# Hashed experts: token rows turned in 32x32 blocks by VectorE, with their quarters loaded on four partition groups

## Chip, cores and metric

The kernel runs on one core of a Trainium2 chip. The metric is the device time in microseconds of one execution; the time given is the median of three runs. The profile is one execution taken by the hardware profiler.

## What is computed

The whole kernel is two layers, each an add of the residual around a conditioned mixture and a second block. The change touches the second layer's mixture only, which picks the expert of a token by a hash:

```
xk = x + dxprev * time_maa_k
e_idx = token_ids * HASH_PRIME % E                       # E = 16 experts
expert_in = buf[:E * C].reshape(E, C, D)                 # C = 256 rows of D = 512 each, scattered from xk
h = square(relu(einsum('ecd,edf->ecf', expert_in, w_key)))       # F = 1024
expert_out = einsum('ecf,efd->ecd', h, w_value)
```

All data is fp32. A product is made of three matmuls on the parts hi and lo of both operands (hi is the operand rounded to fp32r, lo is what is left).

## The kernel before

The program goes through stages, each with its own queues on the engines: shared expert, routed experts, choice, FFN, hashed experts, recurrence. The stages follow each other with a meeting of all engines between them.

**FFN stage.** For each of 32 batches of 128 tokens, POOL computes `xk` in `mix` (L1487; of the last batch VectorE does it in `last_mix`, L1687) and scatters its 128 rows of 2 KB into `hash_in` in DRAM, sorted by expert (L1491). At its end SP loads the first expert's 256 rows as two loads of 128 rows, one row per partition (L1443, `store_r`).

**Hashed stage** (`stage_hashed`). A software pipeline goes over the 16 experts; each engine has a list of stages with a lag, written out by hand, and works through it in that order in each step. `x` holds an expert's rows, `x[:, m]` the 128 rows of half m, with channels along the free axis. TensorE needs channels on partitions, so in step e:

- SP loads w1 of expert e (2 MB, L1902; it waits until w1_lo of the expert before is made), then the two halves of x (L1894; each waits for the semaphore `tx0` or `tx1`, so for its buffer to have been turned), stores half 1 of expert e-2, loads w2 of expert e, a piece of the gate weights, and stores half 0 of e-1.
- TensorE does up(0) to up(3) of expert e-1 (96 matmuls of 256 columns into `h_ps`), then `turn_x(0)` and `turn_x(1)` of expert e (eight 128x128 transposes into the PSUM tiles `tx_ps`, L2077), then down(0) and down(1) of expert e-1 (48 matmuls of 512 columns into `o_ps`). down(0) waits before its chunks k = 0, 2, 4, 6 for w2_lo and for `h_lo(0)`, (1), (2), (3); up(0) waits for both `x_lo` and for all of w1_lo.
- ScalarE makes the hi parts, the relu (`pos`) and the copies out; VectorE the squares (`relu2`, L2031) and the lo parts: `h_lo` (L2037), `x_lo` (L2044), `w1` and `w2` (L2019). Its order is g_lo, w2(0,2), relu2(0), w2(2,3), relu2(1), h_lo(0), w2(3,4), relu2(2), h_lo(1), relu2(3), h_lo(2), h_lo(3), x_lo(0), x_lo(1), w1(0,4).
- In the last step `load_ahead` brings weights of the recurrence into `staged`, and `turn_state` (L2108) turns the first state into `tx_ps[0]`, after `x_lo0`.

Of the kernel before, what the change touches and what calls it, by code (L numbers as in the profile page):

```python
# [13 lines left out]
P = 128  # L14
# [80 lines left out]
def product(pe, out, a, w, first, last):  # L95


    (a_hi, a_lo), (w_hi, w_lo) = a, w
    pe.matmul(out, a_hi, w_hi, start=first, stop=False, skip_group_check=True)  # L99
    pe.matmul(out, a_hi, w_lo, start=False, stop=False, skip_group_check=True)  # L100
    return pe.matmul(out, a_lo, w_hi, start=False, stop=last, skip_group_check=True)  # L101


# [1195 lines left out]
def stage_ffn(nc, ins, d, keep):  # L1299


    with ExitStack() as ctx:
# [80 lines left out]
        def _(sp):  # L1383
# [53 lines left out]
            def store_r(i, n, turn):  # L1437
                b = batch(sp, i)
                if is_last(i):
                    sp.wait_ge(S["mm2"], NB)  # L1440
                    sp.wait_ge(S["xk_sent"], 16 * NB)
                    for m in range(2):
                        sp.dma_start(keep["s5_x"][:, m], d["hash_in"][m * P:(m + 1) * P]).then_inc(S[f"first_hash{m}"], 16)  # L1443
                sp.wait_ge(S["r_ready"], i + 1)
                sp.dma_start(d["r"][b], r[:]).then_inc(S["r_out"], 16)
# [6 lines left out]
        def _(pool):  # L1452
# [21 lines left out]
            def mix(i, n, turn):  # L1474
                if not (isinstance(i, int) and i == NB - 1):
                    pool.wait_ge(S["prev_in"], i * 48 + 48)
                    pool.tensor_tensor(dx[:], prev[:], x1[:], ALU.subtract).then_inc(S["dx"], 1)
                    pool.wait_ge(S["dx"], i + 1)
                    pool.tensor_tensor(k_part[:], dx[:], maa_r[:], ALU.mult).then_inc(S["r_part"], 1)
                    pool.wait_ge(S["r_part"], i + 1)  # L1480
                    wait_for(pool, S["txr"], i)
                    pool.tensor_tensor(xr[:], k_part[:], x1[:], ALU.add).then_inc(S["xr"], 1)
                    pool.wait_ge(S["xr"], i + 1)
                    pool.tensor_tensor(k_part[:], dx[:], maa_k[:], ALU.mult).then_inc(S["k_part"], 1)
                    pool.wait_ge(S["k_part"], i + 1)
                    wait_for(pool, S["xk_sent"], i * 16)
                    pool.tensor_tensor(xk[:], k_part[:], x1[:], ALU.add).then_inc(S["xk"], 1)  # L1487
                pool.wait_ge(S[f"hrec_in{n}"], turn * 16 + 16)
# [112 lines left out]
        def _(dve):  # L1601
# [76 lines left out]
            def last_mix(i, n, turn):  # L1678
                if is_last(i):
# [6 lines left out]
                    dve.wait_ge(S["xk_sent"], (NB - 1) * 16)  # L1686
                    dve.tensor_tensor(xk[:], k_part[:], x1[:], ALU.add).then_inc(S["xk"], 1)  # L1687
                    dve.wait_ge(S["xk"], NB)
# [142 lines left out]
def stage_hashed(nc, ins, d, keep):  # L1831

    with ExitStack() as ctx:  # L1833
        sb = lambda n, s, t=FP32: ctx.enter_context(nc.sbuf_tensor("s5_" + n, s, t))
        ps = lambda n, s, t=FP32: ctx.enter_context(nc.psum_tensor("s5_" + n, s, t))
        S = sems(nc, ctx, "s5_", "w1_in w2_in w1_hi w1_lo w2_hi w2_lo tx0 tx1 x_hi0 x_hi1 x_lo0 x_lo1 "
                 "g_in g_hi g_lo h_ps pos relu h_hi h_lo mm2 o_ready0 o_ready1 ~o_out0 ~o_out1 "
# [29 lines left out]
        NST = 4  # L1867
        staged = right("staged", [P, NST, HS])
        w2_lo = sb("w2_lo", [P, DC, HS], FP32R)

# [7 lines left out]
        h_ps = [ps(f"h_ps{q}", [P, 2, CAP]) for q in range(NQ)]  # L1878
        tx_ps = [ps(f"tx_ps{n}", [P, DC, P]) for n in range(2)]
        o_ps = [ps(f"o_ps{n}", [P, D]) for n in range(2)]  # L1880
# [7 lines left out]
        def _(sp):  # L1888
            def load_x(m):
                def stage(e):  # L1890
                    if isinstance(e, int) and e == 0:
                        return
                    wait_for(sp, S[f"tx{m}"], e)
                    sp.dma_start(x[:, m], d["hash_in"][bass.ds(e * CAP + m * P, P)]).then_inc(S[f"x_in{m}"], 16)  # L1894
                return stage
# [15 lines left out]
            def load_ahead(e):  # L1911
                if isinstance(e, int) and e == EH - 1:
                    sp.wait_ge(F["r_out"], 16 * NB)
                    sp.dma_start(staged[:], ins["gate_w"][0:NST].rearrange("u p n -> p u n")).then_inc(S["u_in"], 16)
                    sp.dma_start(first_rec[:], d["rec"][0]).then_inc(S["rec_in"], 16)
                    for m in range(2):
                        sp.wait_ge(S[f"tx{m}"], EH)
                    sp.dma_start(first_c[:], ins["in_c"].partition_broadcast(P)).then_inc(S["c_in"], 16)
# [20 lines left out]
        def _(act):  # L1939
# [15 lines left out]
            def x_hi_(m):  # L1955
                def stage(e):
                    act.wait_ge(S[f"tx{m}"], e + 1)
                    wait_for(act, S["h_ps"], NQ * e)
                    act.activation(x_hi[:, :, rows(m)], tx_ps[m][:], ACT.Copy).then_inc(S[f"x_hi{m}"], 1)
                return stage  # L1960
# [36 lines left out]
            def state_hi(e):  # L1997
                if isinstance(e, int) and e == EH - 1:
                    act.wait_ge(S["c_turned"], 1)
                    act.wait_ge(S["h_ps"], EH * NQ)  # L2000
                    act.activation(keep["c_hi"][:], tx_ps[0][:], ACT.Copy).then_inc(S["c_hi"], 1)

# [9 lines left out]
        def _(dve):  # L2012
# [21 lines left out]
            def h_lo(q):  # L2034
# [4 lines left out]
                return stage  # L2039

            def x_lo_(m):
                def stage(e):
                    dve.wait_ge(S[f"x_hi{m}"], e + 1)
                    dve.tensor_tensor(x_lo[:, :, rows(m)], tx_ps[m][:], x_hi[:, :, rows(m)],  # L2044
                                      ALU.subtract).then_inc(S[f"x_lo{m}"], 1)
# [11 lines left out]
            def state_lo(e):  # L2057
                if isinstance(e, int) and e == EH - 1:
                    dve.wait_ge(S["c_hi"], 1)
                    dve.tensor_tensor(keep["c_lo"][:], tx_ps[0][:], keep["c_hi"][:], ALU.subtract)  # L2060

# [4 lines left out]
                (1, unit_lo(0, 1)), (1, relu2(2)), (1, h_lo(1)), (1, unit_lo(1, 2)), (1, relu2(3)), (1, h_lo(2)),  # L2066
                (1, h_lo(3)), (1, unit_lo(2, 4)), (1, state_lo), (1, unit_lo(4, UNITS)), (0, x_lo_(0)), (0, x_lo_(1)),
                (0, w1(0, 4))])

        @block.tensor  # L2070
        def _(pe):
            def turn_x(m):
                def stage(e):
                    pe.wait_ge(S[f"x_in{m}"], e * 16 + 16)
                    wait_for(pe, S[f"x_lo{m}"], e)
                    for k in range(DC):
                        mm = pe.transpose(tx_ps[m][:, k], x[:, m, k * P:(k + 1) * P], ident[:])  # L2077
                    mm.then_inc(S[f"tx{m}"], 1)
                return stage

            def up(q):
# [26 lines left out]
            def turn_state(e):  # L2108
                if isinstance(e, int) and e == EH - 1:
                    pe.wait_ge(S["c_in"], 16)  # L2110
                    pe.wait_ge(S["x_lo0"], EH)
                    for k in range(DC):
                        mm = pe.transpose(tx_ps[0][:, k], first_c[:, k * P:(k + 1) * P], ident[:])
                    mm.then_inc(S["c_turned"], 1)

            software_pipeline(pe, EH, [
                (1, up(0)), (1, up(1)), (1, up(2)), (1, up(3)), (1, turn_state), (0, turn_x(0)), (0, turn_x(1)), (1, down(0)),
                (1, down(1))])

# [438 lines left out]
```

## Time and profile before

| | us |
|---|---|
| median of 3 runs | 2510.55 (2509.78 to 2514.25) |
| span of the profiled execution | 2502.9 |
| difference of the two | 7.65 |

The profiled execution's own time outside of its span isn't recorded; the 7.65 us above are between its span and the median of the runs.

| engine | busy us | share of the span |
|---|---|---|
| TensorE matmul | 2451.8 | 98% |
| TensorE weight load | 2046.1 | 82% |
| VectorE | 1148.3 | 46% |
| ScalarE | 897.2 | 36% |
| GpSimd (POOL) | 551.4 | 22% |

The hashed stage runs from about 1466 to 1848 us. Engines are PE (TensorE), PEld (its weight loads), DVE (VectorE), ACT (ScalarE), POOL (GpSimd), SP; SPq is the queue on which SP issues DMAs. A profile shows what an engine was busy with, and in brackets how long it sat idle before and what ended that. An average busy share mixes stages with different limits: what a change in the hashed stage does has to be read from that stage.

### The profile page before, as it was taken

The page shows a single profiled execution, that of the slowest core. Times are in us where ns is not written, and L with a number is a line of the kernel's source. Part 1 is how long each engine was busy: PE and PEld are TensorE (multiplying, and loading weights), DVE is VectorE, ACT ScalarE, POOL GpSimd, SP SyncE. Part 2 cuts the span into 40 slices and gives each one's busy share as a digit, 9 for nine tenths or more (in the row PEclk, how much of TensorE's full clock was granted, in tenths as well). Part 3 has the DMA queues.
Part 4 walks back from the last instruction along what each step waited for, and adds up shares of the span by engine and source line. Part 5 has one row for each costly group of instructions (what it writes and reads, how often), then busy time and mean ns, then how long its engine had stood idle before and what let it go on. Part 6 is the DMA issues. An engine that isn't in the chain of part 4 may idle for free. (4 is left out here: it accounts for less than half of the span.)

```text
span 2502.9 us, 40913 instructions
## 1 busy us (share of the span) xinstructions
PE 2451.8 (98%) x12556; PEld 2046.1 (82%) x12557; DVE 1148.3 (46%) x1771; ACT 897.2 (36%) x1459; POOL 551.4 (22%) x498
## 2 busy tenths in 40 slices
PE   8999999999999899999999989999999999999999
PEld 4778888888899688888888878998978888888877
DVE  5655555325343344344434356766643333332356
ACT  2233333216555222222222246666642222222234
POOL 1100000002222276666657510000011111111100
PEclk9999999999999999999999999999999999999999
DMA  8698898317466433363343266665641011110025
GB/s 297 210 329 310 301 318 317 141 44 269 150 238 223 172 120 111 114 255 108 113 171 127 92 235 230 239 227 222 241 141 43 25 34 30 29 34 25 25 101 185
DMA packets 135988, 412.81 MB, mean 165 GB/s; under 512 B 29843, under 2 KB 34419, under 8 KB 119394
## 3 DMA queue, kind: packets, MB, share of 16 engines
q1 hardware_dynamic: 108626, 314.20, 35.3%
q0 software_dynamic: 19072, 61.66, 7.7%
q10 hardware_dynamic: 8208, 35.88, 3.7%
q8 instruction: 47, 0.77, 0.1%
q14 instruction: 35, 0.29, 0.0%
HBM read 558.71 MB, written 144.80 MB: 281 GB/s over the span
## 5 line engine op out<-in xcount | busy, mean ns | idle before, releaser
L99 PE MATMUL s_g<-wx_hi,s_x_hi 128*128 128x512 f32 x512 | 203.4, 397 | 2.3 <-DVE s_x_lo L2306 1.6
L101 PE MATMUL s_g<-wx_hi,s_x_lo 128*128 128x512 f32 x512 | 200.2, 391 | 0.0
L100 PE MATMUL s_g<-wx_lo,s_x_hi 128*128 128x512 f32 x512 | 199.5, 390 | 0.0
L2019 DVE TENSOR_TENSOR s_w_lo<-s_w_raw,s_w_hi 128x1024 fp32r<-128x1024 f32 x124 | 146.4, 1222 | 75.3 <-ACT s_w_hi L1948 73.7
L99 PE MATMUL s_g<-s_u,s_c_hi 128*128 128x512 f32 x384 | 152.8, 398 | 1.6 <-PEq L1833 1.6
L101 PE MATMUL s_g<-s_u,s_c_lo 128*128 128x512 f32 x384 | 149.9, 390 | 0.0
L100 PE MATMUL s_g<-s_u,s_c_hi 128*128 128x512 f32 x384 | 149.5, 389 | 0.0
L99 PE MATMUL s_h_ps<-s_x_hi,s_w_hi 128*128 128x256 f32 x512 | 144.9, 283 | 1.7 <-DVE s_x_lo L2044 1.7
L101 PE MATMUL s_h_ps<-s_x_hi,s_w_lo 128*128 128x256 f32 x512 | 144.9, 283 | 0.0
L100 PE MATMUL s_h_ps<-s_x_lo,s_w_hi 128*128 128x256 f32 x512 | 144.9, 283 | 0.0
L2205 POOL DMA_INDIRECT s_y<-mid_hash_out,first_rec x32 | 31.6, 986 | 475.4 <-DMA mid_hash_out<-s_o 392.8
L2291 DVE TENSOR_TENSOR s_gate<-s_g,s_bias 128x512 f32<-128x512 f32 x96 | 66.1, 691 | 137.1 <-PE s_g L101 137.1
L1948 ACT ACTIVATE s_w_hi<-s_w_raw 128x1024 fp32r<-128x1024 f32 x124 | 124.1, 1053 | 5.7 <-DMA s_w_raw<-in_w2h 5.7
L394 ACT ACTIVATE s_sg_h<-s_gate 128x512 f32<-128x512 f32 x64 | 38.1, 597 | 245.4 <-PE s_up L101 245.3
L2235 ACT ACTIVATE s_gate<-s_gate 128x512 f32<-128x512 f32 x96 | 60.4, 632 | 175.1 <-DVE s_gate L2291 175.1
L2211 POOL TENSOR_TENSOR s_x<-s_y,s_r 128x512 f32<-128x512 f32 x32 | 44.0, 1374 | 357.4 <-ACT s_r L2223 343.6
L655 DVE TENSOR_TENSOR s_sg_h<-s_sg_h,s_up 128x512 f32<-128x512 f32 x64 | 43.9, 688 | 168.8 <-ACT s_sg_h L394 168.6
L99 PEld LDWEIGHTS s_g<-wx_hi,s_x_hi 128*128 128x128 f32 x512 | 96.2, 188 | 22.5 <-DVE s_x_lo L2306 2.1
L99 PE MATMUL s_gate<-s_xt_hi,s_w_hi 128*128 128x512 f32 x256 | 102.7, 401 | 11.7 <-DVE s_w_lo L472 9.9
L101 PEld LDWEIGHTS s_g<-wx_hi,s_x_lo 128*128 128x128 f32 x512 | 96.1, 188 | 20.9
L100 PEld LDWEIGHTS s_g<-wx_lo,s_x_hi 128*128 128x128 f32 x512 | 96.3, 188 | 19.4 <-issue 0.2
L1555 ACT ACTIVATE s_z_hi<-s_tz_ps 128x512 fp32r<-128x512 f32 x32 | 19.2, 599 | 248.6 <-PE s_tz_ps L1755 248.6
(411 smaller groups left out, 6814.0 us busy)
## 6 DMA issues: line engine op xcount, KB each, us to landing
s_half<-mid_w ACTq DMA_DIRECT2D x124, 2048.0 KB
s_w_raw<-in_w SPq DMA_DIRECT2D x64, 512.0 KB, 6.2
mid_w<-s_x_grp SPq DMA_DIRECT2D x32, 1024.0 KB, 5.8
mid_w<-s_pool_b SPq DMA_DIRECT2D x32, 1024.0 KB, 4.9
s_half<-mid_w SPq DMA_DIRECT2D x32, 1024.0 KB
s_w_raw<-in_w2h SPq DMA_DIRECT2D x16, 2048.0 KB, 7.4
s_w_raw<-in_w1h SPq DMA_DIRECT2D x15, 2048.0 KB, 7.4
mid_routed<-s_o_sb SPq DMA_DIRECT2D x72, 256.0 KB
```

Of the source, the lines that this page charges most:

```text
L99: pe.matmul(out, a_hi, w_hi, start=first, stop=False, skip_group_check=True)
L100: pe.matmul(out, a_hi, w_lo, start=False, stop=False, skip_group_check=True)
L101: return pe.matmul(out, a_lo, w_hi, start=False, stop=last, skip_group_check=True)
L394: act.activation(sg[:, c % 2], gate_ps[c % banks][:], ACT.Silu).then_inc(S["silu"], 1)
L655: dve.tensor_tensor(h[:, c % 2], sg[:, c % 2], up_ps[c % banks][:], ALU.mult).then_inc(S["hmul"], 1)
L1555: act.activation(dst[:], src[:], ACT.Copy).then_inc(S[name], 1)
L1948: act.activation(hi[:, c], raw[:, c], ACT.Copy).then_inc(S[name + "_hi"], 1)
L2019: dve.tensor_tensor(lo[:, c], raw[:, c], hi[:, c], ALU.subtract).then_inc(S[name + "_lo"], 1)
L2205: pool.indirect_dma_start(y[:], None, d["hash_out"], bass.IndirectOffsetOnAxis(rec[:, SLOTH:SLOTH + 1].bitcast(U32), 0)).then_inc(S["y_in" ...
L2211: pool.tensor_tensor(x2[:], y[:], r[:], ALU.mult).then_inc(S["x2"], 1)
L2235: act.activation(gate[:, g], gate[:, g], f).then_inc(S["acted"], 1)
L2291: dve.tensor_tensor(gate[:, g], g_ps[n][g][:], bias[:, g], ALU.add).then_inc(S["added"], 1)
```

## The change

The rows of an expert are no longer turned by TensorE.

- `xk` is written with its columns in another order: quarter g of a row holds columns 32g to 32g+31 of all four 128-column chunks (`by_quarter`), on POOL, and on VectorE for the last batch.
- A half of x is loaded by four DMAs of 32 partitions each, one for each quarter g. Partition 32g + t takes from rows t, 32+t, 64+t, 96+t their quarter g: runs of 512 bytes for 2 KB. They all count on one semaphore (64 for a half in place of 16).
- VectorE's `transpose` of such a tile turns its 32x32 blocks and leaves the channel-major layout in `xt`, in SBUF. `xt` lies on a part of `staged`.
- `turn_x` goes from TensorE's list, where it stood ahead of down(0), to VectorE's, between h_lo(2) and h_lo(3). `x_hi` and `x_lo` read `xt` in SBUF in place of `tx_ps` in PSUM.
- `load_ahead` waits for both `x_lo` of the last expert before it loads `staged`; before, it waited for `tx0` and `tx1`, behind that load. `turn_state` has a PSUM tile of its own, `tc_ps`, and doesn't wait for `x_lo0` any more.

```diff
+def load_by_quarters(eng, dst, rows, sem):
+
+    for g in range(P // 32):
+        eng.dma_start(dst[32 * g:32 * g + 32].rearrange("t (s c) -> t s c", c=P),
+                      rows[:, g * P:(g + 1) * P].rearrange("(s t) c -> t s c", t=32)).then_inc(sem, 16)
+
+
+def in_order(row):
+    return row.rearrange("p (k g a) -> p k g a", k=DC, g=4)
+
+
+def by_quarter(row):
+
+    return row.rearrange("p (g k a) -> p k g a", g=4, k=DC)
+
+
+def turn_quarters(dve, dst, src):
+
+    return dve.transpose(dst.rearrange("p k (s t) -> p k s t", t=32), src.rearrange("p (s k a) -> p k s a", s=4, a=32))
...
-                        sp.dma_start(keep["s5_x"][:, m], d["hash_in"][m * P:(m + 1) * P]).then_inc(S[f"first_hash{m}"], 16)
+                        load_by_quarters(sp, keep["s5_x"][:, m], d["hash_in"][m * P:(m + 1) * P], S[f"first_hash{m}"])
...
-                    pool.tensor_tensor(xk[:], k_part[:], x1[:], ALU.add).then_inc(S["xk"], 1)
+                    pool.tensor_tensor(by_quarter(xk[:]), in_order(k_part[:]), in_order(x1[:]), ALU.add).then_inc(S["xk"], 1)
...
-                    dve.tensor_tensor(xk[:], k_part[:], x1[:], ALU.add).then_inc(S["xk"], 1)
+                    dve.tensor_tensor(by_quarter(xk[:]), in_order(k_part[:]), in_order(x1[:]), ALU.add).then_inc(S["xk"], 1)
...
+        xt = staged[:, 0].rearrange("p (k n) -> p k n", k=DC)
...
-        tx_ps = [ps(f"tx_ps{n}", [P, DC, P]) for n in range(2)]
+        tc_ps = ps("tc_ps", [P, DC, P])
...
-                    wait_for(sp, S[f"tx{m}"], e)
-                    sp.dma_start(x[:, m], d["hash_in"][bass.ds(e * CAP + m * P, P)]).then_inc(S[f"x_in{m}"], 16)
+                    wait_for(sp, S[f"xt{m}"], e)
+                    load_by_quarters(sp, x[:, m], d["hash_in"][bass.ds(e * CAP + m * P, P)], S[f"x_in{m}"])
...
                     sp.wait_ge(F["r_out"], 16 * NB)
+                    for m in range(2):
+                        sp.wait_ge(S[f"x_lo{m}"], EH)
                     sp.dma_start(staged[:], ins["gate_w"][0:NST].rearrange("u p n -> p u n")).then_inc(S["u_in"], 16)
                     sp.dma_start(first_rec[:], d["rec"][0]).then_inc(S["rec_in"], 16)
-                    for m in range(2):
-                        sp.wait_ge(S[f"tx{m}"], EH)
...
-                    act.wait_ge(S[f"tx{m}"], e + 1)
+                    act.wait_ge(S[f"xt{m}"], e + 1)
                     wait_for(act, S["h_ps"], NQ * e)
-                    act.activation(x_hi[:, :, rows(m)], tx_ps[m][:], ACT.Copy).then_inc(S[f"x_hi{m}"], 1)
+                    act.activation(x_hi[:, :, rows(m)], xt[:, :, rows(m)], ACT.Copy).then_inc(S[f"x_hi{m}"], 1)
...
+            def turn_x(m):
+                def stage(e):
+                    dve.wait_ge(S[f"x_in{m}"], e * 64 + 64)
+                    wait_for(dve, S[f"x_lo{m}"], e)
+                    turn_quarters(dve, xt[:, :, rows(m)], x[:, m]).then_inc(S[f"xt{m}"], 1)
+                return stage
...
-                    dve.tensor_tensor(x_lo[:, :, rows(m)], tx_ps[m][:], x_hi[:, :, rows(m)],
+                    dve.tensor_tensor(x_lo[:, :, rows(m)], xt[:, :, rows(m)], x_hi[:, :, rows(m)],
...
-                (1, h_lo(3)), (1, unit_lo(2, 4)), (1, state_lo), (1, unit_lo(4, UNITS)), (0, x_lo_(0)), (0, x_lo_(1)),
+                (0, turn_x(0)), (0, turn_x(1)), (1, h_lo(3)), (1, unit_lo(2, 4)), (1, state_lo), (1, unit_lo(4, UNITS)), (0, x_lo_(0)), (0, x_lo_(1)),
...
-            def turn_x(m):
-                def stage(e):
-                    pe.wait_ge(S[f"x_in{m}"], e * 16 + 16)
-                    wait_for(pe, S[f"x_lo{m}"], e)
-                    for k in range(DC):
-                        mm = pe.transpose(tx_ps[m][:, k], x[:, m, k * P:(k + 1) * P], ident[:])
-                    mm.then_inc(S[f"tx{m}"], 1)
-                return stage
...
-                    pe.wait_ge(S["x_lo0"], EH)
...
-                (1, up(0)), (1, up(1)), (1, up(2)), (1, up(3)), (1, turn_state), (0, turn_x(0)), (0, turn_x(1)), (1, down(0)),
+                (1, up(0)), (1, up(1)), (1, up(2)), (1, up(3)), (1, turn_state), (1, down(0)),
```

## Rows read from the trace of the kernel before

**Rows 1.** Windows: busy time and count per engine in one step, clock, DMA share, GB/s
```profile
1693.00:1716.60 23.60, 23.60 (x155) 21.44 (x153) 16.26 (x19) 14.63 (x21) 0.00 (x0) 1.00 0.61 230
```
**Rows 2.** Chain that ended last: start, us, what; two steps
```profile
1693.30 0.87 PE s_tx_ps L2077 x8
...
1716.88 0.87 PE s_tx_ps L2077 x8
```
**Rows 3.** Timeline of TensorE (start, us, instruction), from up to down to up
```profile
1693.01 0.28 PE L101 MATMUL s_h_ps<-s_x_hi,s_w_lo 128*128 128x256 f32 x1
...
1693.13 1.03 PE L2077 MATMUL s_tx_ps<-ident,s_x 128*128 128x128 f32 x8
...
1693.92 0.48 PE L99 MATMUL s_o_ps<-s_w_hi,s_ht_hi 128*128 128x512 f32 x1
...
1694.24 0.39 PE L100 MATMUL s_o_ps<-s_w_lo,s_ht_hi 128*128 128x512 f32 x1
...
1705.20 0.28 PE L99 MATMUL s_h_ps<-s_x_hi,s_w_hi 128*128 128x256 f32 x1
```
**Rows 4.** Timeline of VectorE: first expert, then the same step as rows 3
```profile
1483.00 1.47 DVE L2037 TENSOR_TENSOR s_ht_lo<-s_h,s_ht_hi 128x512 fp32r<-128x512 f32 x2
...
1694.05 0.69 DVE L2031 TENSOR_TENSOR s_h<-s_pos,s_h_ps 128x512 f32<-128x512 f32 x1 [1.59 <-ACT s_pos L1966]
1694.66 1.48 DVE L2037 TENSOR_TENSOR s_ht_lo<-s_h,s_ht_hi 128x512 fp32r<-128x512 f32 x2
1696.05 1.28 DVE L2044 TENSOR_TENSOR s_x_lo<-s_tx_ps,s_x_hi 128x512 fp32r<-128x512 f32 x2
1697.36 4.63 DVE L2019 TENSOR_TENSOR s_w_lo<-s_w_raw,s_w_hi 128x1024 fp32r<-128x1024 f32 x4
```
**Rows 5.** Timeline of ScalarE in that step
```profile
1694.77 0.63 ACT L1973 ACTIVATE s_ht_hi<-s_h 128x512 fp32r<-128x512 f32 x1 [0.32 <-DVE s_h L2031]
```
**Rows 6.** Timeline of VectorE and TensorE in the last expert, where TensorE waits
```profile
1837.05 0.68 DVE L2031 TENSOR_TENSOR s_h<-s_pos,s_h_ps 128x512 f32<-128x512 f32 x1
1837.65 1.47 DVE L2037 TENSOR_TENSOR s_ht_lo<-s_h,s_ht_hi 128x512 fp32r<-128x512 f32 x2
...
1838.48 0.47 PE L99 MATMUL s_o_ps<-s_w_hi,s_ht_hi 128*128 128x512 f32 x1 [0.47 <-DVE s_ht_lo L2037]
1838.79 0.39 PE L100 MATMUL s_o_ps<-s_w_lo,s_ht_hi 128*128 128x512 f32 x1
```
**Rows 7.** Timeline of SP's queue, and DMA issues (count, KB each, us to landing)
```profile
1702.69 0.86 SPq L1894 DMA_DIRECT2D s_x<-mid_hash_in  x2
...
s_x<-mid_hash_in SPq DMA_DIRECT2D x30, 256.0 KB, 7.7
```
**Rows 8.** Start of the stage: timelines, and the landing of L1443's two loads
```profile
1460.07 0.83 SPq L1443 DMA_DIRECT2D s_x<-mid_hash_in  x2
...
DMA to landing us min/median/max: 2.6/2.8/2.9
...
1466.28 1.06 PE L2077 MATMUL s_tx_ps<-ident,s_x 128*128 128x128 f32 x8 [1.75 <-PEq L1302]
...
1466.94 1.09 ACT L1959 ACTIVATE s_x_hi<-s_tx_ps 128x512 fp32r<-128x512 f32 x2 [1.78 <-PE s_tx_ps L2077]
...
1469.01 0.36 PE L99 MATMUL s_h_ps<-s_x_hi,s_w_hi 128*128 128x256 f32 x1 [1.66 <-DVE s_x_lo L2044]
```
**Rows 9.** Windows around the stage's start, columns as rows 1
```profile
1457.00:1460.00 3.00, 0.74 (x5) 0.51 (x5) 3.00 (x4) 2.26 (x3) 0.86 (x1) 1.00 0.47 175
1460.00:1462.00 2.00, 2.00 (x6) 1.59 (x7) 2.00 (x2) 0.23 (x1) 0.00 (x0) 0.61 0.37 110
...
1464.00:1469.00 5.00, 1.60 (x11) 0.97 (x10) 1.29 (x2) 1.68 (x3) 0.00 (x0) 1.00 0.50 147
```
**Rows 10.** Timeline of POOL in the FFN stage
```profile
1198.46 1.30 POOL L1487 TENSOR_TENSOR s_xk<-s_k_part,s_x 128x512 f32<-128x512 f32 x1 [0.16 <-POOL s_k_part L1484]
...
1204.44 0.96 POOL L1460 DMA_INDIRECT s_routed<-mid_routed,s_rec  x1 [2.78 <-DVE s_y_part L1643]
```

More of the change, by code:

```diff
@@ L1835, in stage_hashed @@
         ps = lambda n, s, t=FP32: ctx.enter_context(nc.psum_tensor("s5_" + n, s, t))
-        S = sems(nc, ctx, "s5_", "w1_in w2_in w1_hi w1_lo w2_hi w2_lo tx0 tx1 x_hi0 x_hi1 x_lo0 x_lo1 "
+        S = sems(nc, ctx, "s5_", "w1_in w2_in w1_hi w1_lo w2_hi w2_lo xt0 xt1 x_hi0 x_hi1 x_lo0 x_lo1 "
                  "g_in g_hi g_lo h_ps pos relu h_hi h_lo mm2 o_ready0 o_ready1 ~o_out0 ~o_out1 "
@@ L2000, in state_hi @@
                     act.wait_ge(S["h_ps"], EH * NQ)
-                    act.activation(keep["c_hi"][:], tx_ps[0][:], ACT.Copy).then_inc(S["c_hi"], 1)
+                    act.activation(keep["c_hi"][:], tc_ps[:], ACT.Copy).then_inc(S["c_hi"], 1)
             w1 = lambda c0, c1: split_w("w1", w1_raw, w1_hi, "h_ps", NQ, c0, c1)
@@ L2059, in state_lo @@
                     dve.wait_ge(S["c_hi"], 1)
-                    dve.tensor_tensor(keep["c_lo"][:], tx_ps[0][:], keep["c_hi"][:], ALU.subtract)
+                    dve.tensor_tensor(keep["c_lo"][:], tc_ps[:], keep["c_hi"][:], ALU.subtract)
             w1 = lambda c0, c1: split_w("w1", w1_raw, w1_hi, w1_lo, c0, c1)
@@ L2110, in turn_state @@
                     pe.wait_ge(S["c_in"], 16)
-                    pe.wait_ge(S["x_lo0"], EH)
                     for k in range(DC):
-                        mm = pe.transpose(tx_ps[0][:, k], first_c[:, k * P:(k + 1) * P], ident[:])
+                        mm = pe.transpose(tc_ps[:, k], first_c[:, k * P:(k + 1) * P], ident[:])
                     mm.then_inc(S["c_turned"], 1)
             software_pipeline(pe, EH, [
-                (1, up(0)), (1, up(1)), (1, up(2)), (1, up(3)), (1, turn_state), (0, turn_x(0)), (0, turn_x(1)), (1, down(0)),
+                (1, up(0)), (1, up(1)), (1, up(2)), (1, up(3)), (1, turn_state), (1, down(0)),
                 (1, down(1))])
```

## The prediction

> **What bounds the kernel now.** I read the windows first: in one expert's step of the hashed stage TensorE is busy 23.60 of 23.60 us at full clock, VectorE 16.26, ScalarE 14.63 [rows 1]. The chain of the end comes back in every step to the eight transposes of `turn_x` [rows 2]. So TensorE alone sets the step, and what leaves its queue is won unless something else becomes late. The timeline then gives the step's parts [rows 3]: the last up matmul starts at 1693.01, the transposes at 1693.13, the first down matmul at 1693.92, the next at 1694.24, and the next expert's up, 47 down matmuls on, at 1705.20. Down matmuls follow each other every (1705.20 - 1694.24)/47 = 0.233 us; the one behind the transposes takes 0.32, which is 0.09 more. From 1705.20 the next 96 up matmuls take about 11.5 us, and the period is 23.58 (the two chain rows).
>
> **Removed from TensorE.** 1693.92 - 1693.13 = 0.79 us of transposes, plus the 0.09 after them if the 128-column transposes cause it: 0.79 to 0.88 per step, I take 0.87, since 0.233 is what each of the 46 others takes. Sixteen pairs of transposes exist; the first stands alone at the stage's start, fifteen lie between an up and a down.
>
> **Added to VectorE, and what waits for it.** Two turns now stand between `h_lo(2)` and `h_lo(3)`, and down(0) needs `h_lo(3)` for its chunks k=6 and 7. Before, `relu2(3)` starts at 1694.05 and `h_lo(2)` at 1694.66 [rows 4]; back to back such instructions follow each other every 0.60 to 0.61 us though each shows 0.68 (1837.05 to 1837.65, [rows 6]), so the next slot is at 1694.66 + 0.61 = 1695.27. ScalarE's `h_hi(3)` ends by 1694.77 + 0.63 = 1695.40 [rows 5] and is out of the way. With T for one turn, `h_lo(3)` ends at 1695.27 + 2T + 0.68. TensorE answers 0.14 us later: `h_lo(2)` of the last expert ends at about 1837.65 + 0.68 = 1838.33 and the matmul that waited starts at 1838.48; that one also takes 0.31 to the next, 0.08 too long [rows 6]. So the matmul is possible at 1696.09 + 2T. It is due, with the transposes gone, 18 matmuls after 1693.13: 1693.13 + 18 x 0.233 = 1697.33. The stall per step is 2T - 1.24, plus 0.08 if it is above zero: 2T - 1.16.
>
> No VectorE transpose is in the profile. Lower end: a turn costs what any 128x512 instruction does, 0.61. Upper end: twice the columns' time, as a 128x1024 instruction, (4.63 us for four) 1.16 [rows 4]. I take 0.65, near the lower row, because it reads and writes the same 512 elements per partition; the surplus 0.04 is for filling and emptying the blocks. The stall is then 0.14 and the net gain 0.87 - 0.14 = 0.73 per step.
> The Trainium skill ("VectorE: DVE Perf Modes", The three transpose paths) gives 311 ns for a 128x128 bf16 transpose on VectorE, in 32x32 blocks. With the columns of a 1x instruction (the rows' 1.16 less 0.61 for 512 columns, 1.07 ns each) 311 ns is 137 for the columns and 174 of fixed cost, near the 0.68 - 0.55 = 0.13 of our rows, so by it the turn would show 0.72 and pass in 0.65 if fp32 goes as fast as bf16; no run here shows that yet. The same page's rules for kernel authors send a 128x128 transpose to TensorE when PSUM will do; by that rule the change gives up 0.79 us of TensorE for at least 1.22 of VectorE, and the sum goes by which of the two is waited for.
>
> **The first two steps.** In the first expert VectorE runs late: `h_lo(2)` starts at 1483.00, 2.5 us after the end of the up phase and not 1.5 as later [rows 4]. TensorE would be due for k=6 at 1469.01 + 96 x 0.12 + 4.2 = 1484.7; `h_lo(3)` would be ready at 1483.61 + 1.30 + 0.68 + 0.14 = 1485.7. The stall of 1.0 eats the 0.87: this step gives nothing. At the stage's start the transposes (1466.28) give `x_hi` at 1466.94 and the first up matmul at 1469.01 [rows 8]. With turns from the same moment, the second ends at 1467.6, `x_hi(1)` at 1468.3, `x_lo(1)` at 1469.0, up starts at 1469.15: 0.15 late.
>
> **Sum.** 14 steps x 0.73 = 10.2; step one 0; start -0.15: 10.0 us less. The trace has only the span (2502.9); the runs' median is 2510.55, 7.65 above it, and their three values spread over 4.5. I take the difference off the median: 2500.5 (span 2492.9).
>
> **What I cost at nothing, and its cover.** (1) w1's low halves now end later: `h_lo(3)` slot ends 1697.2, two `x_lo` 1698.4, four `w1_lo` (4.63, [rows 4]) 1703.1. Up is due at 1693.13 + 0.14 + 11.2 = 1704.5: 1.3 us of cover, 3 before; without it each late us costs 15. ScalarE's `x_hi` now reads SBUF, and its four w1 copies start about 1 us later; they stay ahead of VectorE's, which are slower. (2) SP: two loads of 256 KB become eight of 64 KB. Both took 0.86 us to issue, 0.43 each [rows 7]; eight take 3.4. They stand behind w1 and ahead of `store(1)`, w2 and gate loads. w1 goes out about 1.1 us later (its gate is `w1_lo`), the pieces from 1703.8 to 1707.3, and landing at the 7.7 of [rows 7], most of which is w1's own 2 MB ahead of them, 1715.0. The turn wants them at 1695.27 + 22.85 = 1718.1: cover 3.1 us. What stands behind in SP's queue (`store(1)`) has a whole step before its buffer is reused. On VectorE the turn's wait holds `h_lo(3)`, `x_lo` and w1, and with them TensorE: nothing if the cover holds. Packets of 512 B for 2 KB cost between nothing and four times the landing of a load alone: 2.8 [rows 8] to 11.2, 8.4 more, which would pass the cover. I take under 1, because these loads spend most of their time behind w1. (3) The first eight loads start at 1460.07 and are issued by 1463.5, landed by 1466.4 with 2.9 [rows 8], the moment the turns begin; the r store behind them in SP's queue waits for TensorE's last products anyway. (4) `xk` is written in runs of 32 elements: POOL takes 1.30 for it now and idles 2.78 ahead of its next gather [rows 10]; between no change and twice (+1.3) nothing waits. The last batch's is VectorE's, 0.69, on the path: 0 to 0.1. (5) The staged load now waits for `x_lo` of the last expert, done 9 us before SP gets there behind `store(1)`. (6) `turn_state` has its own bank and one wait less; its four transposes stay.
>
> **Rivals.**
> *A, forecast*: 2500.5; with T from 0.61 to 0.75 the steps give 0.81 to 0.53, hence 2499.2 to 2503.3. Chance 0.45.
> *B, the clock falls at the start.* At 1460 to 1462 the granted clock was 0.61 (between the levels 1.2 and 2.4 GHz), after TensorE had been busy 0.74 of 3.00 us; at 1464 to 1469 it held 1.00 with 1.60 of 5.00 busy, 1.06 of it the transposes that go [rows 9]. Without them 0.54 of 5.15 remains. A fall costs what it did there, matmuls 0.42 apart for about 3.3 us, 8 x 0.19 = 1.5 us: 2502.0. Chance 0.20.
> The Trainium skill ("TensorE: Matmul & The Clock Gate", Part 4) says transposes do not count as TensorE being busy in the same way; by it the clock would do now as it did before, and B falls. The rows can't separate the two.
> *C, slower: the turn takes twice as long.* The gain is gone when 2T - 1.16 = 0.87, T = 1.01. At T = 1.16 the stall is 1.16 and each of 14 steps loses 0.29 (4.1), step one another 1.2, the start 1.2, likely with B's 1.5: 8 us, 2518.5. For it: 4-byte data turned in blocks with a strided source, shown nowhere here. Against: the same bytes in and out as its neighbours. Chance 0.12.
> *D, slower: the pieces land late.* From 3.1 us beyond the old landing each us costs 15; at the far bound, (8.4 - 3.1) x 15 = 80, 2590. Against: the DMA share of a step is only 0.61 [rows 1]. Chance 0.05.
> The Trainium skill ("DMA: Bandwidth & Descriptors", Measured) calls transfers under 64 KB descriptor-dominated and asks for large ones; by it the pieces at 64 KB are at the edge, and D is what it would do here.
> *E, the gain is smaller:* the turn at 0.85 to 0.95, or TensorE's switch of sizes keeps its 0.09 and waking costs more: 0.1 to 0.4 per step, 2505 to 2509. Chance 0.18.
>
> **Range and chances.** Faster by over 0.2% (5.0 us, about what a measurement can tell from no change) means below 2505.5: A, B and some of E, 0.68. Within: most of E, and little of C, 0.17. Slower: most of C and D, 0.15. 2498.5 to 2510 holds A, B and E, leaves out C and D.
>
> **What would show it.** In the profile after: no `s_tx_ps` matmuls at the old line, chain and step period 22.85 in place of 23.58; VectorE's turns 0.7 us long, `h_lo(3)` ending at 4.1 us after the up phase's end; TensorE idle about 0.15 a step before k=6, released by `s_ht_lo`; up never waiting for `w_lo`; VectorE never waiting for DMA before a turn. A turn above 1.0, a wait for `s_x`, or up waiting for w1 makes the prediction wrong; a fallen clock near 1469 moves it to B.

## The result, and the profile after

| | before | after |
|---|---|---|
| median, us | 2511.51 (2509.78 to 2514.25, 4 runs) | 2496.77 (2495.91 to 2497.94, 4 runs) |
| ratio | | 0.9945, interval 0.9931 to 0.9958 |
| span of the profiled execution, us | 2502.9 | 2494.3 |
| period of the hashed stage, us | 23.58 | 22.72 |

The kernel got 14.7 us faster; 10.0 had been forecast, and 2496.77 lies below the range. The direction and the place are as predicted, the size isn't. Of the runs that are quoted further on, one of the changed kernel took 3496.12 us at a mean granted clock of 0.65 in place of 0.99; no ratio counts it.

The windows of the kernel after, in one step of the hashed stage; columns as in [rows 1]:

```profile
1693.00:1715.70 22.70, 22.70 (x146) 20.45 (x145) 17.27 (x23) 14.81 (x22) 0.00 (x0) 1.00 0.68 236
```

TensorE is still busy in all of it. VectorE rose from 16.26 to 17.27. The timeline of TensorE, from the up matmuls to the first down matmul and on to the next up, answers [rows 3]:

```profile
1689.49 0.28 PE L101 MATMUL s_h_ps<-s_x_hi,s_w_lo 128*128 128x256 f32 x1
1689.61 0.39 PE L99 MATMUL s_o_ps<-s_w_hi,s_ht_hi 128*128 128x512 f32 x1
1689.84 0.39 PE L100 MATMUL s_o_ps<-s_w_lo,s_ht_hi 128*128 128x512 f32 x1
...
1700.80 0.28 PE L99 MATMUL s_h_ps<-s_x_hi,s_w_hi 128*128 128x256 f32 x1
```

The first down matmul comes 0.12 us behind the last up matmul; it was 0.91 before (1693.92 - 1693.01). The next follows after 0.23, not 0.32. So the 0.79 of transposes and most of the 0.09 behind them are gone. The waits of TensorE from 1440 to 1850 us (engine, what it was to do, what it waited for: total, times, longest) show no wait that comes back in every step:

```profile
PE s_h_ps L99 <- DVE s_x_lo L2073: 4.6, 1, 4.6
...
PE s_o_ps L99 <- DVE s_ht_lo L2059: 0.5, 1, 0.5
```

The second stands in the last expert, as it did before [rows 6]. VectorE's timeline in the same step answers [rows 4]:

```profile
1690.53 0.69 DVE L2053 TENSOR_TENSOR s_h<-s_pos,s_h_ps 128x512 f32<-128x512 f32 x1 [1.59 <-ACT s_pos L1988]
1691.13 0.69 DVE L2059 TENSOR_TENSOR s_ht_lo<-s_h,s_ht_hi 128x512 fp32r<-128x512 f32 x1
1691.74 1.30 DVE L122 STREAM_TRANSPOSE s_staged<-s_x 128x512 f32<-128x512 f32 x2
1692.96 0.65 DVE L2059 TENSOR_TENSOR s_ht_lo<-s_h,s_ht_hi 128x512 fp32r<-128x512 f32 x1
1693.53 1.28 DVE L2073 TENSOR_TENSOR s_x_lo<-s_staged,s_x_hi 128x512 fp32r<-128x512 f32 x2
1694.73 4.62 DVE L2041 TENSOR_TENSOR s_w_lo<-s_w_raw,s_w_hi 128x1024 fp32r<-128x1024 f32 x4
```

The two turns take the queue for 1692.96 - 1691.74 = 1.22 us, 0.61 each. `h_lo(3)` ends at 1693.61 and TensorE could go on 0.14 later, at 1693.75. The down matmul that needs it is the 19th, due at 1689.61 + 18 x 0.233 = 1693.80. By these ends it fits with 0.05 us to spare. The matmul itself does start when it is due, but the one behind it doesn't:

```profile
1693.80 0.42 PE L99 MATMUL s_o_ps<-s_w_hi,s_ht_hi 128*128 128x512 f32 x1
1694.06 0.39 PE L100 MATMUL s_o_ps<-s_w_lo,s_ht_hi 128*128 128x512 f32 x1
```

It follows after 0.26 in place of 0.23. The same 0.26 or 0.27 stands behind the first matmul of k=6 in every step from the third to the fifteenth. So the slack is used up, and a first 0.02 to 0.03 of a stall shows.

### Where the two traces differ

I put anchors into both traces and measured between them: the last batch's `x1` on VectorE in the FFN stage (an instruction that the change leaves alone), the first up matmul, the first down matmul, the second expert's up, the last expert's up, and the recurrence's first matmul.

| stretch, us | before | after | difference |
|---|---|---|---|
| start to `x1` of the last batch | 1450.37 | 1452.66 | +2.29 |
| to the first up | 18.64 | 18.77 | +0.13 |
| to the first down | 12.70 | 13.72 | +1.02 |
| to the second expert's up | 11.28 | 11.18 | -0.10 |
| 14 steps | 330.11 | 318.09 | -12.02 |
| last up to the recurrence | 25.63 | 25.66 | +0.03 |
| recurrence to the end | 654.17 | 654.22 | +0.05 |

Fourteen steps give 12.0; the forecast had 10.2 there. The spans differ by only 8.6, since this trace of before is of a short execution: 2502.9 of span where its runs take 2511.5, while the time outside the span is 1.6 (2495.91 for a span of 2494.3 after), and not the 7.65 between this span and the median. Two rows of the table, 2.29 and 1.02, therefore had to be told from the change. The second is TensorE's clock, in the windows of after (answering [rows 9]):

```profile
1471.00:1473.00 2.00, 1.57 (x7) 1.60 (x8) 0.28 (x1) 0.00 (x0) 0.00 (x0) 0.50 0.99 418
...
1475.00:1477.00 2.00, 2.00 (x14) 2.00 (x14) 0.00 (x0) 0.40 (x1) 0.00 (x0) 0.68 1.06 451
```

After an idle stretch of 4.6 us the first up matmuls run at the lower level, 1.2 GHz, 0.21 apart, where they ran 0.12 apart in the trace of before. That looks like rival B. Whether the change causes it is what the first three experiments ask.

### The profile page after: what moved, and what is told of

It reads as the page before. It is cut to its first block and busy times, and to the rows that moved or that the text cites. A ratio compares the mean times of both kernels' runs of the same rounds, so it can differ in the third digit from the quotient of the medians.

```text
span 2494.3 us, 40938 instructions
## 1 busy us (share of the span) xinstructions
PE 2440.2 (98%) x12427; PEld 2033.9 (82%) x12429; DVE 1165.9 (47%) x1803; ACT 900.0 (36%) x1459; POOL 552.1 (22%) x498
## 5 line engine op out<-in xcount | busy, mean ns | idle before, releaser
L99 PE MATMUL s_gate<-s_xt_hi,s_w_hi 128*128 128x512 f32 x256 | 103.0, 402 | 12.9 <-DVE s_w_lo L493 9.9
```

## The experiments

The first theory (theory 1 in the expectations) was that the gain is the whole of TensorE's 0.86 us per step, with VectorE's turns just fitting in, and that what is seen at the stage's start belongs to the executions and not to the change. Against it stood that the missing transposes let the clock fall (B), that part of the gain comes from the loads or from other places than TensorE's queue, and that the stall of 2T - 1.24 + 0.08 is there but hidden by something else.

### The two kernels again, and the transposes put back

The kernel before ran once more as it is, so did the changed kernel, and a third kernel is the changed one with eight transposes (of the identity, into a spare PSUM tile) in TensorE's queue at their old place:

```diff
+            def spare_turns(e):
+                for m in range(2):
+                    for k in range(DC):
+                        pe.transpose(tc_ps[:, k], ident[:], ident[:])
-                (1, up(0)), (1, up(1)), (1, up(2)), (1, up(3)), (1, turn_state), (1, down(0)),
+                (1, up(0)), (1, up(1)), (1, up(2)), (1, up(3)), (1, turn_state), (0, spare_turns), (1, down(0)),
```

> The kernel before, unchanged, against itself. The traces of before and after differ by 8.6 us in span, the medians of the runs by 14.7; trace by trace, 10.9 of it lies in the hashed stage and 2.3 went the other way ahead of it. Theory 1: the change acts in the hashed stage alone, and the missing 4 us is how much one execution of the same program differs from another ahead of that stage: ratio 1.000 within 0.001, and the spans of the single executions spread over some 4 us, with 2502.9 at their low end. Theory 2: the 14.7 is real and has a part outside of the hashed stage that this trace doesn't show: the spans of before lie close together at about 2509, and a new trace shows where the 4 us are.

> The changed kernel, unchanged, in five rounds. Theory 1 (in-stage effect of 10.9 us only): 11 us under before, ratio 0.9957. Theory 2 (another part outside): 14.7 under it, ratio 0.9942.

> The changed kernel with eight 128x128 transposes of the identity put back on TensorE where turn_x stood (results unused), everything else as changed. Theory 1 (the gain is TensorE's time alone, 0.86 per step with the 0.09 of the switch): the period goes back from 22.72 to 23.58, and the time to that of before, within 1 us. Rival (part of the gain comes from the loads by quarters or from reading SBUF in place of PSUM): the period stays below 23.4 and the time 3 us or more under before.

| | median, us | ratio to before | period | first up to first down |
|---|---|---|---|---|
| before (25 runs beside them) | 2507.97 | | | |
| before again | 2508.38 | 1.0002 (0.9993 to 1.0011) | 23.58 | 15.05 |
| after again | 2495.38 | 0.9952 (0.9938 to 0.9966) | 22.72 | 14.15 |
| after, transposes put back | 2508.94 | 1.0001 (0.9991 to 1.0010) | 23.58 | 14.99 |

The timeline of TensorE in the kernel with the transposes put back, in one step:

```profile
1721.44 1.04 PE L2138 MATMUL s_tc_ps<-ident 128*128 128x128 f32 x8
1722.23 0.48 PE L99 MATMUL s_o_ps<-s_w_hi,s_ht_hi 128*128 128x512 f32 x1
1722.55 0.39 PE L100 MATMUL s_o_ps<-s_w_lo,s_ht_hi 128*128 128x512 f32 x1
```

They bring back 0.79 us and the 0.32 after them, and with these the old period of 23.58 to the hundredth and the old time. The new loads, the turns on VectorE and the other layout of `xk` are all still in that kernel, so together they cost and give nothing that these runs can tell (the interval is 0.1% to each side, 2.5 us; the period is the finer measure). POOL's `xk`, written in runs of 32 elements, takes 1.301 us on average with and without the change, and VectorE's 0.69. The gain is TensorE's time. The unchanged kernel agrees with itself at 1.0002, but its single executions spread from 2503.4 to 2513.4, 10 us and not the 4 that theory 1 had.

The window of the unchanged kernel in its second trace, where its first up matmuls stand:

```profile
1472.00:1474.00 2.00, 2.00 (x11) 2.00 (x11) 0.00 (x0) 0.00 (x0) 0.00 (x0) 0.50 1.00 426
```

The clock falls there too, with eight transposes that start 2.7 us earlier and an idle stretch of 1.67 after them. It held in one execution of this kernel and fell in another; it fell as well with the transposes put back. So the fall comes without the change too, and it doesn't need the transposes to be gone. The Trainium skill ("TensorE: Matmul & The Clock Gate", Part 4) says that transposes don't count as a busy TensorE in the same way; these two traces fit that, the lower level came in spite of eight transposes, but in the first trace of before it didn't come.

Whether the change makes the fall more frequent is another question, and it stays open. The clock fell in all seven traces of kernels that have neither the transposes nor spare matmuls there, and in two of three with the transposes. The mean granted clock of whole runs points the same way, though other stretches enter into it: it is 0.995 or more in 28 of 64 runs of the unchanged kernel, in 3 of 10 with the transposes put back, and in none of 14 of the changed kernel. Against B, the fall isn't the change's alone; as a cost of the change B isn't refuted.

Like for like the first step now reads: 15.05 + 11.28 against 14.15 + 11.17, 1.0 us less. With the 12.0 of the steps and 0.15 to 0.2 lost at the start the stage gains 12.8. Against the execution of before in which the clock held, the changed kernel's first step (24.90 to 25.40 in three traces, 23.98 before) loses 0.9 to 1.4, and the stage gains 10.7 to 10.9.

### The turn's price

Each turn is done twice, the first time into a spare tile; then the same for half 0 alone:

```diff
+        spare = staged[:, 1].rearrange("p (k n) -> p k n", k=DC)
...
+                turn_quarters(dve, spare[:, :, rows(m)], x[:, m])
                 turn_quarters(dve, xt[:, :, rows(m)], x[:, m]).then_inc(S[f"xt{m}"], 1)
```

> The changed kernel with each VectorE turn done twice, the first into an unused tile. By the prediction's working with T = 2 x 0.61, h_lo(3) ends 1.22 later than in the changed kernel, the matmul of k=6 is possible 1.20 after it is due, plus 0.08 for waking: 1.28 per step, 15 steps 19 us, start 1.2: 20 us above the changed kernel, so 5 to 9 above before; TensorE idles at s_ht_lo every step. Rival (VectorE's place in front of h_lo(3) is not what counts, there is more slack than computed): under 5 us above the changed kernel.

> The changed kernel with only the turn of half 0 done twice: 0.61 us more on VectorE per step. With both twice (1.22 more) the period went from 22.72 to 23.90, so the slack ahead of h_lo(3) in the changed kernel would be 1.22 - 1.18 = 0.04 us. If the step is a wait that grows one for one from that slack, the period is 22.72 + 0.61 - 0.04 = 23.29 and the time 8.5 us above the changed kernel. Rival: waking TensorE has a fixed price and the slack is larger; then the period is 23.35 or more, or under 23.2.

All turns twice: 2513.36 us, ratio 1.0024 (1.0014 to 1.0035), 18.0 above the changed kernel of the same comparison; period 23.82 to 23.91. Half 0 twice: 2507.22, ratio 0.9985 (0.9976 to 0.9994), mean period 23.28. TensorE's waits, and then VectorE's timeline, with all turns doubled:

```profile
PE s_o_ps L99 <- DVE s_ht_lo L2060: 15.0, 16, 1.0
```

```profile
1703.33 2.48 DVE L122 STREAM_TRANSPOSE s_staged<-s_x 128x512 f32<-128x512 f32 x4
1705.73 0.65 DVE L2060 TENSOR_TENSOR s_ht_lo<-s_h,s_ht_hi 128x512 fp32r<-128x512 f32 x1
```

The same two views with half 0 doubled:

```profile
PE s_o_ps L99 <- DVE s_ht_lo L2060: 6.1, 16, 0.5
```

```profile
1700.74 1.89 DVE L122 STREAM_TRANSPOSE s_staged<-s_x 128x512 f32<-128x512 f32 x3
1702.56 0.65 DVE L2060 TENSOR_TENSOR s_ht_lo<-s_h,s_ht_hi 128x512 fp32r<-128x512 f32 x1
```

Four turns take 2.40, three 1.82, two 1.22: 0.60 to 0.61 each. The period rises by 0.56 with one turn more (23.28 - 22.72) and by 1.17 with two (mean 23.89), so of the added 0.60 and 1.18 all but 0.04 and 0.01 is paid. From the changed kernel on VectorE's time is paid one for one. This is the stall of the forecast's formula. It exists, and it begins where the change put the kernel. Its two parts show in the traces: with half 0 doubled, in the step of the timeline above, the matmul of k=6 starts at 1703.35, 0.54 after it is due, and the next follows 0.31 later, 0.08 too long:

```profile
1703.35 0.47 PE L99 MATMUL s_o_ps<-s_w_hi,s_ht_hi 128*128 128x512 f32 x1 [0.38 <-DVE s_ht_lo L2060]
1703.66 0.39 PE L100 MATMUL s_o_ps<-s_w_lo,s_ht_hi 128*128 128x512 f32 x1
```

### The turns behind h_lo(3)

If a stall were left in the changed kernel, moving the turns behind `h_lo(3)` would take it away.

```diff
-                (0, turn_x(0)), (0, turn_x(1)), (1, h_lo(3)), (1, unit_lo(2, 4)), ...
+                (1, h_lo(3)), (0, turn_x(0)), (0, turn_x(1)), (1, unit_lo(2, 4)), ...
```

> The changed kernel with both turns on VectorE behind h_lo(3) in place of ahead of it. The slack ahead of h_lo(3) is some 0.04 us in the changed kernel and the stall zero; with the turns behind it the slack is 1.2 us and nothing else waits, so the period stays 22.72 and the time that of the changed kernel within 1 us. Rival: w1_lo, now later still (x_lo waits for x_hi, which waits for the turn), passes its cover of 1.3 us: the period grows.

2498.00 us, ratio 0.9947 (0.9933 to 0.9962), beside 2496.44 and 0.9947 (0.9934 to 0.9959) for the changed kernel in the same comparison. The period is 22.70 against 22.72: 0.3 us in 14 steps. Behind the first matmul of k=6 the next now follows after 0.23 or 0.24, so this 0.02 is what the changed kernel pays of the stall. Nothing more is left to win there. `h_lo(3)` is ready 1.2 us earlier, and the order costs nothing in the period either, though `x_lo` and the w1 copies now wait for ScalarE: the copies end at 1703.53, 0.69 ahead of up at 1704.22, where the changed kernel has 1.45.

> The changed kernel once more, on the chip of the two variants. Theory: the effect in the hashed stage is 12.0 for 14 steps, and 1.0 for step one when the clock is low in both kernels; 12.8 in all, and what a comparison shows beyond is the spread ahead of that stage: ratio 0.995 within 0.001.

### The loads in pieces

The eight pieces of a step become two loads of 128 rows of 2 KB. The layout is left as it then falls, so what the experts are fed is wrong, but every instruction except the loads is the same:

```diff
-    for g in range(P // 32):
-        eng.dma_start(dst[32 * g:32 * g + 32].rearrange("t (s c) -> t s c", c=P),
-                      rows[:, g * P:(g + 1) * P].rearrange("(s t) c -> t s c", t=32)).then_inc(sem, 16)
+    eng.dma_start(dst, rows).then_inc(sem, 16)
...
-                    dve.wait_ge(S[f"x_in{m}"], e * 64 + 64)
+                    dve.wait_ge(S[f"x_in{m}"], e * 16 + 16)
```

> The changed kernel with each half of x loaded by one DMA of 128 rows of 2 KB again, in place of four of 512-byte runs; the rows then lie in the wrong places for the turn, so the expert's input isn't the reference's, and every instruction's size stays. If the pieces cost nothing (they are covered by 3 us and more), period and time are those of the changed kernel within 1 us. Rival: the pieces disturb the stage's start or the w1 load: this kernel is 2 us or more faster.

2499.21 us (2495.22 to 2506.88), ratio 0.9955 (0.9942 to 0.9968), period 22.72. (In its trace the first up stands 0.9 us later behind `x1` than in the changed kernel's, 19.63; one trace doesn't say whether that is the edit or the execution.) The DMA issues from 1500 to 1850 us (what, how many, KB each, us to landing), in pieces and then whole:

```profile
s_x<-mid_hash_in SPq DMA_DIRECT2D x104, 64.0 KB, 6.5
```

```profile
s_x<-mid_hash_in SPq DMA_DIRECT2D x27, 256.0 KB, 7.7
```

The pieces cost nothing that shows: the period is the same to the hundredth and the median not lower (it was expected within 1 us of the changed kernel's, 2496.77, and is 2.4 above it, with runs that spread over 11.7). A piece lands 6.5 us after its issue, a whole load 7.7. The pieces of a step are complete later all the same, since the last is issued 3.7 us after the first; VectorE waits for neither. D is refuted. The Trainium skill ("DMA: Bandwidth & Descriptors", Measured) calls transfers under 64 KB descriptor-dominated; pieces of just 64 KB in runs of 512 B show no price in this kernel.

### The clock at the start

Could the lower clock in the first up phase be bought back? Ten spare matmuls of 512 columns fill TensorE's idle stretch:

```diff
+            for n in range(10):
+                pe.matmul(tc_ps[:].rearrange("p k n -> p (k n)"), w1_hi[:, 0, 0:P], w1_hi[:, 0, 0:D],
+                          start=True, stop=True, skip_group_check=True)
             software_pipeline(pe, EH, [
```

A second kernel has six more at the end of the FFN stage, a third has the ten with the turns behind `h_lo(3)`:

> The changed kernel with ten matmuls of 512 columns (results unused) at the very start of the hashed stage, while VectorE turns. If the clock falls because TensorE idles in the stage's start, the first up matmuls run at 0.12 in place of 0.21: 2.35 us less to the first down, some of it lost because VectorE is then late for k=6 in step one (about 1.0): 1.3 under the changed kernel. Rival: the fall is decided ahead of the stage, in the idle time after the FFN stage's last product: no change, or worse, since the ten matmuls then take 4.3 us and delay up.

> As the kernel with ten spare matmuls at the start of the hashed stage, and six more behind the last product of the FFN stage, in the time in which the engines meet. If the idle time between the stages decides, the clock holds here at 1.00 and the gain of 1.3 to 2.3 under the changed kernel shows; if the clock was lost by then already in the FFN stage's last batch, nothing does.

> Ten spare matmuls at the stage's start, and the turns behind h_lo(3). With the clock held, step one showed a stall: 12.37 us from the first down matmul to up of expert 1, for 11.18. That stall is the turns ahead of h_lo(3) while VectorE is late; behind it, 11.2 to 11.3 should come back, 1.1 us less than with the ten matmuls alone, and 2.4 less than the changed kernel. Rival: the stall is w2's late arrival itself and stays.

| | median, us | ratio to before | `x1` to first up | first up to first down | to second up |
|---|---|---|---|---|---|
| after (its first trace) | 2496.77 | 0.9945 | 18.77 | 13.72 | 11.18 |
| ten spare matmuls | 2496.47 | 0.9944 (0.9929 to 0.9959) | 18.78 | 11.57 | 12.37 |
| with six more ahead | 2498.99 | 0.9950 (0.9936 to 0.9963) | 19.91 | 12.51 | 12.39 |
| ten, turns behind `h_lo(3)` | 2495.85 | 0.9946 (0.9933 to 0.9959) | 18.49 | 12.75 | 12.21 |

The last row stands in a later comparison than the two above it, in which before had 2509.34 and not 2511.01. The kernel with ten: the window of its first up matmuls, TensorE's timeline at the first wait of the down phase, and VectorE's timeline in that step:

```profile
1476.00:1478.00 2.00, 2.00 (x19) 2.00 (x18) 0.00 (x0) 0.00 (x0) 0.00 (x0) 1.00 1.04 438
```

```profile
1488.18 0.47 PE L99 MATMUL s_o_ps<-s_w_hi,s_ht_hi 128*128 128x512 f32 x1 [0.70 <-DVE s_ht_lo L2059]
```

```profile
1480.40 2.36 DVE L2041 TENSOR_TENSOR s_w_lo<-s_w_raw,s_w_hi 128x1024 fp32r<-128x1024 f32 x2 [6.25 <-ACT s_w_hi L1970]
...
1490.37 0.65 DVE L2059 TENSOR_TENSOR s_ht_lo<-s_h,s_ht_hi 128x512 fp32r<-128x512 f32 x1
```

The clock held, and the up phase got 2.15 us shorter. But 1.19 of it is lost again in the down phase, in waits for `h_lo` before k=2 (the line above) and before k=6, where TensorE goes on at 1491.17, 0.15 after the end of `h_lo(3)`. VectorE starts this expert's w2 copies at 1480.40 in any case: they wait for ScalarE's, and these for the first w2, as ScalarE's timeline in this kernel says:

```profile
1479.32 2.01 ACT L1970 ACTIVATE s_w_hi<-s_w_raw 128x1024 fp32r<-128x1024 f32 x2 [5.90 <-DMA s_w_raw<-in_w2h]
```

So with the clock held the first expert is bound by w2's landing. A TensorE that is quicker there waits later. In the third kernel, with the turns out of the way too, TensorE waits for `h_lo` earlier, 1.01 us before its first down matmul and 0.70 before k=2: 12.75 + 12.21 = 24.96 against 13.72 + 11.18 = 24.90. That isn't the work of the order, since the second kernel, with the turns ahead of `h_lo(3)`, has nearly the same two waits (0.76 and 0.70) and 24.90. In both traces w2 came later: ScalarE starts on it 8.9 and 8.7 us after its issue, 7.7 in the trace with ten. Six more spare matmuls in the FFN stage delay the first up by 1.1 us. The ten were expected to give 1.3 us and the third kernel 2.4; no variant is faster than the changed kernel by more than its runs spread.

The same two traces test the first step of the forecast. Clock high in both, [rows 9] and the ten spare matmuls: 12.70 + 11.28 = 23.98 before and 11.57 + 12.37 = 23.94 after. The step gives nothing, as forecast, because the late VectorE eats what is saved. (The 1.13 saved in the up phase is more than 0.87, since in this one execution 1.24 us passed between the last up and the first down matmul, where the other steps have 0.91.) Clock low in both: 1.0 us, because a slower TensorE meets its `h_lo(3)` in time.

## Why the prediction was right, and where it was not

The time came out 3.7 us below the forecast and 1.7 below its range. Of the 3.7, the stall per step, the term that failed, accounts for 1.8, and the first step for 1.0. About 1 is left; the traces don't show it in the hashed stage, and its cause stays open.

**What leaves TensorE: right.** 0.87 forecast, 0.86 measured (23.58 - 22.72), and again 0.86 when the transposes were put back. The 0.09 behind the transposes did belong to them.

**The turn's price and the stall: mechanism right, size off.** This is the term that failed: "2T - 1.16" with T = 0.65, 0.14 per step, 2.0 us in 14. Measured is 0.02 per step, 0.3 us in 14, and no idle time before k=6. Two things were wrong in it. T is 0.61: the turn shows 0.69 and passes in 0.61 like any 128x512 neighbour of it; the 0.04 for "filling and emptying the blocks" had no row behind it. The prediction's estimate from the 311 ns of the Trainium skill ("VectorE: DVE Perf Modes", The three transpose paths) was 0.72 shown and 0.65 spaced if fp32 went as fast as bf16; the trace has 0.686 and 0.61, a little less than that estimate. And the 0.08 for waking TensorE was put into the formula without its condition, though the text named it ("plus 0.08 if it is above zero"): with T = 0.61 the stall is 1.22 - 1.24, just below zero, and but for the 0.02 neither part is paid. The range for A did start at T = 0.61, but 2T - 1.16 gives 0.06 there, and so its 2499.2 was too high: without a stall the same sum gives 2510.55 - 14 x 0.87 + 0.15 = 2498.5. (The 2499.2 also leaves out the 0.15 of the start, which the range's upper end, 2503.3, has.) The runs with three and four turns confirm the slope of the formula, not its constant: against the 22.70 without a stall they add 0.58 and 1.19 to the period, and the formula with their 1.82 and 2.40 on VectorE in place of 2T gives 0.66 and 1.24. It is 0.05 to 0.08 too high, about the price that it sets for waking.

**The first step: right at a high clock, wrong at a low one.** 0 was forecast (0.87 saved, 1.0 waited) from a trace in which the clock held, and with the clock held it is 0.04 (1.13 saved in the up phase, 1.09 lost behind it). It fell in the other trace of before and in every trace of the changed kernel without spare matmuls. With the fall in both kernels the step gives 1.0. I took the clock of one execution at the stage's start for the kernel's.

**The start: right.** 0.15 late forecast; 0.13 in the first pair of traces, 0.18 in the second (18.61 against 18.43).

**The covers: right.** Up waits for no w1: the four copies end at 1699.35 (1694.73 + 4.62), 1.45 ahead of up at 1700.80, 1.3 forecast. The pieces land in time. `xk` costs nothing more on POOL. The issue of the pieces was under-priced, 0.50 each and not 0.43 (SP's queue in the same step, the second line), without consequence:

```profile
1699.51 0.33 SPq L1924 DMA_DIRECT2D s_w_raw<-in_w1h  x1
1700.04 4.01 SPq L107 DMA_DIRECT2D s_x<-mid_hash_in  x8
```

**The rivals.** B: the clock did fall, as the sign said it would, but it falls without the change as well; against an execution of before in which it held, the fall costs 0.9 to 1.4, near the 1.5 of the forecast. C: T is 0.61, not 1.16; the runs with all turns done twice, 1.20 for a pair, show what C would have been: 2513.36, 18.0 above the changed kernel, as far as C's 2518.5 lies above the forecast. D: no. E: the switch of sizes didn't keep its 0.09, and waking cost 0.02 a step at most.

**The sum.** With the terms as measured (12.0 + 1.0 - 0.2) it is 12.8 us, 2497.8 from 2510.55. The differences of medians in three comparisons are 14.7, 12.6 and 12.9. The kernel before had medians of 2511.51, 2507.97, 2511.01 and 2509.34 in four of them, with single runs from 2503.4 to 2514.3. The stretch ahead of the stage also differs, with POOL's `xk` as the one thing changed in it, which takes as long as before: `x1` of the last batch stands at 1450.37 and 1452.37 in the two traces of before, and between 1452.66 and 1456.07 in those of the other kernels. So 12.8 of the 14.7 is explained by the stage where the clock falls in both kernels. The other 1.9 is within the spread of the base. Part of that spread goes with the clock: the unchanged kernel's runs at a mean granted clock of 0.993 or 0.994 average 2510.3 (34 of them), those at 0.995 or 0.996 average 2507.6 (28). The changed kernel's 14 runs all have 0.993 or 0.994 and average 2496.2. That is 14.1 and 11.4 less, beside 12.8 to 13.1 and 10.7 to 10.9 by the stage in the pairs of traces. About 1 us is left over in either; I didn't test it, and it stays open whether it belongs to the change. The forecast's range had no term for this spread; its low end, 2498.5, was just the sum without a stall.

## What to carry to other kernels

When an engine is busy in the whole of a step, what leaves its queue is won in full, as long as the engine that takes it over has slack in front of the one result that is waited for; compute the slack to the hundredth, and charge a stall (and the price of waking) only where it comes out above zero. Close to zero such a sum is good to some hundredths of a us per step, and the range should say so. For an operation that the trace doesn't show, take the pitch of the nearest neighbour with the same bytes and let the range, not the value, carry the doubt. Before a term is taken from a stage's start or end, look at more than one execution: here the granted clock and the stretch ahead differed from one to the next by 2 us each.

## What was new about the hardware

- A 128x512 fp32 transpose in 32x32 blocks, read in runs of 32 elements and written in runs of 128 (SBUF to SBUF), costs VectorE the same as a subtraction of that size: 0.686 us shown (0.667 to 0.711, 32 of them), 0.60 to 0.61 from one to the next.
- Eight fp32 128x128 transposes cost TensorE 0.79 us and 0.07 to 0.09 more at the next 512-column matmul; taking them out between two kinds of fp32r matmul gave both back.
- TensorE's clock at the start of a stage, after some us of little work, was 1.00 in one execution and 0.50 in another of the same kernel. The lower level cost 2.35 us in the up phase of the kernel before (15.05 against 12.70) and 2.15 to 2.66 in that of the changed one (13.72 to 14.23 against 11.57). In the kernel before all of it stayed; in the changed one only 1.0 to 1.5 (24.90 to 25.40 against 23.94 to the second up), since a quicker TensorE waits for VectorE there.
- The single executions of one kernel spread over 10 us of 2508, and the slower ones have the lower mean granted clock: 2510.3 on average at 0.993 and 0.994, 2507.6 at 0.995 and 0.996 (62 runs). That one is the cause of the other wasn't tested.
